# Multi-level attention with a feed-forward network: side products of TensorE in two parts

## The chip, the cores and the metric

One core of a Trainium2 chip runs the whole kernel. The time is that of one execution on the device in microseconds (us). Engines: TensorE (PE; its weight loads are PEld), VectorE (DVE), ScalarE (ACT), GpSimd (POOL), SyncE (SP, which starts most transfers).

## What is computed

The input is x of shape (8, 1024, 256) in float32. Cut to what matters:

```
for lvl in range(4):                       # strides 1, 2, 4, 8
    xs = x[:, ::2**lvl, :]                 # 1024, 512, 256, 128 tokens
    outs.append(mha(xs, in_proj_w[lvl], in_proj_b[lvl], out_w[lvl], out_b[lvl]))   # 16 heads of 16
current = outs[3]
for lvl in (2, 1, 0):
    current = upsample_linear(current, 2x) @ up_w[lvl].T + up_b[lvl] + outs[lvl]
x = layernorm(x + current)
h = silu(x @ w1 * s1) * (x @ w2 * s2)      # 256 -> 1024
h = gelu(h @ h1 * t1);  h = gelu(h @ h2 * t2)
x = layernorm(x + h @ w3 * s3)
```

## The kernel before

The program has two parts: attention for all eight batches (`attention`), and the feed-forward network (`ffn`). The change touches the first alone.

**Units and steps.** Attention of a batch is cut into 15 units, each of a level, four heads (more on the coarse levels, which have fewer tokens) and 512 queries. A unit runs over the key tiles of 128 tokens; one key tile is a step, and a batch has 85 steps (`STEPS`). A step has four maximum products ("max", L1313, 48 rows of the array each), two pairs of score products ("score", L1300, 50 rows each), and eight value products ("value", L1330). The maxima run 12 steps ahead of the scores (`LEAD`): VectorE reduces each of them out of PSUM (L1086), and the row maxima go into the scores as additional rows of the operands. ScalarE takes the exponentials of two score banks at a time (L982), and the value products of step s are issued two steps later.

**Rows of the array.** Heads lie in the upper or the lower 64 partitions (`rows_of`). Max 0 and max 2 of a fine step are in one half, max 1 and max 3 in the other (`maxima_of`), and each score pair has one product in either half.

**Side products.** Everything else that TensorE does in attention has a place at the end of a step (`SIDE = .85`): projections of q and k ("proj", 15 a batch), value projections ("v", 8), output products of the three coarse levels ("mid", 4), the up-projections ("lift", 2, and "row", 2), output products of the fine level ("out", 4), and transposes of the row maxima ("neg", 15). Apart from "neg" each is made of float32 operands cut into a high and a low part, three matmuls per product and 128 rows (`three`, L1190). Most have six matmuls of 512 columns or twelve of 256; the projections of level 3 are 24 of 128 columns.

**What sets the order.** `timeline` gives every task a time in steps, with the fraction as its place within the step. Each engine issues its tasks sorted by that time, with the engine's own additions in `LATER`. In a step TensorE thus has max 0 (.0), max 1 (.05), value (.1), max 2 (.3), score 0 (.4), max 3 (.6), score 1 (.7) and then the side product (.85). The order is unrolled for one batch, with a hardware loop over it, an opening ahead of it (the first batch's projections and maxima) and an end behind it.

**The ring.** Maxima and side products share three PSUM banks (`p_r`, `BANKS = 3`). `bank_plan` goes through them in order of time and gives each the bank that is promised free first; `HOLD` says for how long each kind keeps one (.45 of a step for a maximum, .7 to 1.1 for the others). Before TensorE writes into a bank it waits until the bank's last user was read: by VectorE for "max", "v", "row" and "out", by ScalarE for "proj", "neg", "mid" and "lift". The scores have four banks of their own and the value products one.

```
bank = min(range(BANKS), key=lambda bank: held[bank][0])
plan.bank[tuple(task)], plan.prev[tuple(task)] = bank, held[bank][1]
held = held[:bank] + [(at + HOLD[task[0]], [tuple(task)])] + held[bank + 1:]
```

Of the kernel before, what the change touches and what calls it, by code (L numbers as in the profile page):

```python
# [79 lines left out]
PROJ = [[Proj(2, t, m, 0) for t in range(2)] for m in range(2)]  # L80
# [3 lines left out]
PROJ_FIRST = {lvl: min(n for n, ps in enumerate(PROJ) if ps[0].lvl == lvl) for lvl in W_ORDER}  # L84
# [40 lines left out]
V_PAIRS = [[n for n, (l, kt) in enumerate(V_ORDER) if l == lvl][i:i + 2] for lvl in W_ORDER for i in range(0, tokens(lvl) // 128, 2)]  # L125
V_FIRST = {lvl: [ns[0] for ns in V_PAIRS].index(V_TILE[lvl]) for lvl in W_ORDER}
# [13 lines left out]
MID_FIRST, MID_DONE = {3: 0, 2: 1, 1: 2}, {3: 1, 2: 2, 1: 4}  # L140
# [92 lines left out]
def earlier(it):  # L233
# [30 lines left out]
def timeline(first):  # L264

    p = []
# [4 lines left out]
    side = places([(("neg", u), unit.end - LEAD) for u, unit in enumerate(UNITS)], taken)  # L271
# [9 lines left out]
    for lvl in W_ORDER:  # L281
# [5 lines left out]
        else:  # L287
# [17 lines left out]
    if first:  # L305
        at = [side[("proj", n)] for n in range(len(PROJ))]
# [86 lines left out]
def attention(nc, xt_in, xtok, wqkv_in, wo_in, cols, rows, ident_in, xt, wqkv, wo, scr, d75s, d25s, x1, wf, hi_scr, lo_scr, lo_max, f_hi, f_w3_lo):  # L393
# [31 lines left out]
    def bank_plan(p, held):  # L425

        plan = Plan({}, {})
        for at, *task in sorted(p, key=lambda task: (task[0], task[1:])):
            if task[0] in HOLD:
                bank = min(range(BANKS), key=lambda bank: held[bank][0])  # L430
                plan.bank[tuple(task)], plan.prev[tuple(task)] = bank, held[bank][1]
                held = held[:bank] + [(at + HOLD[task[0]], [tuple(task)])] + held[bank + 1:]
        return plan, held

    def one_batch_on(held):
# [12 lines left out]
    with ExitStack() as ctx:  # L448
# [153 lines left out]
        with nc.Block() as block:  # L602
# [573 lines left out]
            def _(pe):  # L1176
# [6 lines left out]
                lift_mm.open(pe)  # L1183
                row_mm.open(pe)

                def three(out, pairs):

                    terms = [t for (a_h, a_l), (b_h, b_l) in pairs for t in ((a_h, b_h), (a_l, b_h), (a_h, b_l))]
                    for n, (a, c) in enumerate(terms):
                        ins = pe.matmul(out, a, c, start=n == 0, stop=n == len(terms) - 1)  # L1190
                    return ins

                def both(hi, lo, *at):

                    return hi[at], lo[at]
# [1 line left out]
                every = slice(None)  # L1197

                def steps(tasks, iteration, plan):
                    for task in tasks:  # L1200
                        kind, k, n = task
                        it = iteration(k)
                        if kind in HOLD:
                            p_a = p_r[:, plan.bank[task], :]
                        for was, at, m in plan.prev.get(task, ()):

                            {"max": max_read, "proj": qk_read, "neg": neg_read, "v": v_done, "mid": mid_read, "lift": lift_read, "row": row_read, "span": span_read,
                             "out": out_read}[was].wait(pe, iteration(at), m + 1)
                        if kind == "proj":
                            lvl = PROJ[n][0].lvl  # L1210
                            size = min(W, tokens(lvl))
                            if n == 0:
                                x_lo_done.wait(pe, it, 1)
                            if n == PROJ_FIRST[0]:
                                x_lo_done.wait(pe, it, 2)
                            if n == PROJ_FIRST[lvl]:
                                w_lo_done.wait(pe, it, W_ORDER.index(lvl) + 1)
                            for i, (_, t, m, blk) in enumerate(PROJ[n]):
                                tok = slice(blk * W, blk * W + size)
                                ins = three(p_a[:, i * size:(i + 1) * size],  # L1220
                                            [(both(w_hi, w_lo, every, slice(at, at + 128)), both(x_hi, x_lo, every, c, tok))
                                             for c in range(2) for at in (c * 512 + t * 256 + m * 128,)])
                            ins.then_inc(qk_mm.sem, 1)
                        elif kind == "neg":
                            if n < FIRST_FINE:
                                max_read.wait(pe, it, MAX_AT[n + 1])
# [3 lines left out]
                                ins = pe.transpose(p_a[0:HG, q * 128:(q + 1) * 128], row_max[:, n % RING, q, :], ident[:, :])  # L1230
                            ins.then_inc(neg_mm.sem, 1)
                        elif kind == "v":
                            if n == V_FIRST[0]:
                                x_lo_done.wait(pe, it, 2)
                            for i, tile in enumerate(V_PAIRS[n]):
# [4 lines left out]
                            ins.then_inc(v_mm.sem, 1)  # L1240
                        elif kind == "mid":
                            lvl, ms = MIDS[n]
                            S, at = tokens(lvl), A_AT[lvl]
                            if n == MID_FIRST[lvl]:
                                a_lo_done.wait(pe, it, CUT_DONE[lvl])
                                o_lo_done.wait(pe, it, O_ORDER.index(lvl) + 1)
                            for i, m in enumerate(ms):
                                ins = three(p_a[:, i * S:(i + 1) * S], [(both(o_hi, o_lo, every, slice(c * E + m * 128, c * E + m * 128 + 128)),
                                                                         both(a_hi, a_lo, every, c, slice(at, at + S))) for c in range(2)])
                            ins.then_inc(mid_mm.sem, 1)  # L1250
                        elif kind == "lift":
                            lvl = O_ORDER[n]
                            S, at = tokens(lvl), A_AT[lvl]
                            c_lo_done.wait(pe, it, n + 1)
                            for m in range(2):
                                ins = three(p_a[:, m * S:(m + 1) * S], [(both(o_hi, o_lo, every, slice(WUP + c * E + m * 128, WUP + c * E + m * 128 + 128)),
                                                                         both(a_hi, a_lo, every, c, slice(at, at + S))) for c in range(2)])
                            ins.then_inc(lift_mm.sem, 1)
                        elif kind == "row":
                            if n == 0:  # L1260
# [5 lines left out]
                            ins.then_inc(row_mm.sem, 1)  # L1266
                        elif kind == "out":
                            if n % 2 == 0:
                                a_lo_done.wait(pe, it, len(CUTS) - 1 + n // 2)
                            if n == 0:  # L1270
                                o_lo_done.wait(pe, it, 4)
                            for q in range(2):
# [3 lines left out]
                            ins.then_inc(out_mm.sem, 1)  # L1276
# [533 lines left out]
```

## Time and profile before

| what | us |
| --- | --- |
| median of 3 runs | 4003.92 |
| lowest and highest | 3999.56, 4011.51 |
| profiled execution | 4005.5 |
| its span, first to last instruction | 4003.7 |
| TensorE busy in the span | 3642.2 (91%) |
| ScalarE busy | 2595.1 (65%) |
| VectorE busy | 2552.1 (64%) |

The page's slices cut the span into 40 equal parts of about 100 us; each digit is a busy share in tenths. The windows view gives, for one or more stretches of time, the busy time of each engine in it with the number of its instructions, the granted TensorE clock, and the DMA's share and rate; its last row sums over all stretches and divides by their number. Where a group below has a row that begins with "sum", the stretches were chosen by one rule, which the group's line names, over 300 to 2600 us, and what stands for one step is that sum divided by the number of stretches.

### The profile page before, as it was taken

The page shows a single profiled execution, that of the slowest core. Times are in us where ns is not written, and L with a number is a line of the kernel's source. Part 1 is how long each engine was busy: PE and PEld are TensorE (multiplying, and loading weights), DVE is VectorE, ACT ScalarE, POOL GpSimd, SP SyncE. Part 2 cuts the span into 40 slices and gives each one's busy share as a digit, 9 for nine tenths or more (in the row PEclk, how much of TensorE's full clock was granted, in tenths as well). Part 3 has the DMA queues.
Part 4 walks back from the last instruction along what each step waited for, and adds up shares of the span by engine and source line. Part 5 has one row for each costly group of instructions (what it writes and reads, how often), then busy time and mean ns, then how long its engine had stood idle before and what let it go on. Part 6 is the DMA issues. An engine that isn't in the chain of part 4 may idle for free. (4 is left out here: it accounts for less than half of the span.)

```text
span 4003.7 us, 70655 instructions
## 1 busy us (share of the span) xinstructions
PE 3642.2 (91%) x20993; PEld 1954.6 (49%) x20993; DVE 2552.1 (64%) x4806; ACT 2595.1 (65%) x3273; POOL 1051.4 (26%) x1024
## 2 busy tenths in 40 slices
PE   5899889989989989989988988869999999999998
PEld 3333333333333323333333332258878787887887
DVE  5778978878878887887897898523333333333333
ACT  2779778868868868877877978734444344443443
POOL 2233434434444343343443342210000000000000
PEclk6989989989989989998998999979999999999999
DMA  4423423422332332333332344210000000000000
GB/s 138 156 70 98 123 77 91 118 81 86 105 95 87 105 107 79 103 95 93 89 117 72 99 123 135 75 51 12 12 12 13 21 11 12 12 11 13 21 11 11
DMA packets 231920, 284.40 MB, mean 71 GB/s; under 512 B 53524, under 2 KB 189908, under 8 KB 230384
## 3 DMA queue, kind: packets, MB, share of 16 engines
q1 hardware_dynamic: 222272, 270.54, 22.5%
q10 hardware_dynamic: 9216, 8.39, 0.6%
q8 instruction: 236, 3.87, 0.4%
q14 instruction: 196, 1.61, 0.1%
HBM read 166.63 MB, written 108.00 MB: 69 GB/s over the span
## 5 line engine op out<-in xcount | busy, mean ns | idle before, releaser
L982 ACT ACTIVATE a_probs<-a_p_s,a_unit_now 128x1024 f32<-128x1024 f32 x1360 | 1448.7, 1111 | 351.9 <-PE a_p_s L1300 345.3
L1086 DVE TENSOR_REDUCE a_part_max<-a_p_r 128x1 f32<-128x512 f32 x2048 | 1301.6, 676 | 270.9 <-PE a_p_r L1313 266.4
L1313 PE MATMUL a_p_r<-a_k_st,a_q_st 48*128 48x512 f16 (+2 forms) x2944 | 921.0, 383 | 209.5 <-DVE a_part_max L1086 126.2
L1313 PEld LDWEIGHTS a_p_r<-a_k_st,a_q_st 48*128 48x128 f16 x2944 | 229.1, 94 | 1239.6 <-DVE a_part_max L1086 871.3
L1642 PE MATMUL p_h<-f_h_hi,f_w_hi 128*128 128x512 f32 x2048 | 807.3, 394 | 24.0 <-issue 24.0
L1642 PE MATMUL p_h<-f_h_lo,f_w_hi 128*128 128x512 f32 x2048 | 803.2, 392 | 0.0
L1330 PE MATMUL a_p_o<-a_probs,a_v_aug 128*17 128x512 f32 (+2 forms) x5888 | 747.5, 588 | 3.5 <-ACT a_raw L992 2.8
L1300 PE MATMUL a_p_s<-a_q_st,a_k_st 50*128 50x512 f16 (+2 forms) x2944 | 694.9, 376 | 25.9 <-ACT a_probs L982 24.0
L1613 DVE TENSOR_TENSOR f_h_lo<-f_h_f,f_h_hi 128x512 fp32r<-128x512 f32 x256 | 177.1, 692 | 697.2 <-ACT f_h_hi L1539 697.2
L1537 ACT ACTIVATE f_h_f<-p_h,f_sc 128x512 f32<-128x512 f32 x256 | 176.6, 690 | 556.7 <-PE p_h L1642 556.6
L1086 DVE TENSOR_REDUCE a_row_max<-a_p_r 128x1 f32<-128x512 f32 (+2 forms) x672 | 427.2, 676 | 98.2 <-PE a_p_r L1313 95.9
L1642 PEld LDWEIGHTS p_h<-f_h_hi,f_w_hi 128*128 128x128 f32 x2048 | 388.5, 190 | 107.9 <-issue 26.4
L1642 PEld LDWEIGHTS p_h<-f_h_lo,f_w_hi 128*128 128x128 f32 x2048 | 388.6, 190 | 80.1
L1483 POOL TENSOR_TENSOR f_rstd<-f_var_eps,f_minus_half 128x1 f32<-128x1 f32 x64 | 35.6, 556 | 1325.9 <-DVE f_var_eps L1604 1325.9
L837 POOL TENSOR_TENSOR a_qk_room<-a_qk_room 128x512 f16<-128x512 f32 x114 | 132.1, 1159 | 381.3 <-ACT a_qk_room L969 381.3
L859 POOL TENSOR_TENSOR a_neg_bf<-a_neg_f,a_neg_bf 4x512 f16<-4x512 f32 x120 | 138.3, 1153 | 308.8 <-ACT a_neg_bf L976 308.8
L1642 PE MATMUL p_h<-f_xt_hi,f_w_hi 128*128 128x512 f32 x512 | 200.3, 391 | 1.4 <-DVE f_xt_lo L1565 1.4
L1642 PE MATMUL p_h<-f_xt_lo,f_w_hi 128*128 128x512 f32 x512 | 200.1, 391 | 0.0
L1300 PEld LDWEIGHTS a_p_s<-a_q_st,a_k_st 50*128 50x128 f16 x2944 | 155.7, 95 | 90.1 <-ACT a_probs L982 59.7
L1581 DVE SCALAR_TENSOR_TENSOR f_h_f<-p_h,f_sc,f_gate 128x512 f32<-128x512 f32 x128 | 96.1, 751 | 158.6 <-PE p_h L1642 138.8
L1330 PEld LDWEIGHTS a_p_o<-a_probs,a_v_aug 128*17 128x17 f32 x5888 | 105.4, 96 | 175.0 <-issue 121.9
L863 POOL TENSOR_TENSOR a_attn<-a_raw,a_attn 128x512 f32<-128x512 f32 x120 | 152.9, 1274 | 126.5 <-DVE a_attn L1138 126.5
(131 smaller groups left out, 4533.6 us busy)
## 6 DMA issues: line engine op xcount, KB each, us to landing
qk_scratch<-a_qk_room SPq DMA_DIRECT2D x288, 128.0 KB
a_w_lo<-wqkv_inner SPq DMA_DIRECT2D x30, 768.0 KB, 4.3
a_q_st<-qk_scratch SPq DMA_DIRECT2D x64, 192.0 KB, 3.7
a_k_st<-qk_scratch SPq DMA_DIRECT2D x64, 192.0 KB, 4.8
a_a_lo<-a_attn SPq DMA_DIRECT2D x384, 32.0 KB, 2.0
a_o_lo<-wo_inner SPq DMA_DIRECT2D x24, 512.0 KB, 3.7
a_qk_room<-wf SPq DMA_DIRECT2D x22, 512.0 KB, 3.8
w_lo_scratch<-a_qk_room SPq DMA_DIRECT2D x22, 512.0 KB, 2.7
```

The costliest lines, as they stand in the source:

```text
L837: pool.tensor_tensor(out=pieces[:, 1, :], in0=qk[:, 0:size], in1=pieces[:, 0, :], op=ALU.subtract).then_inc(qk_lo.sem, 1)
L859: pool.tensor_tensor(out=neg_bf[:, n % 2, 1, :], in0=neg_f[:, :], in1=neg_bf[:, n % 2, 0, :], op=ALU.subtract).then_inc(neg_b.sem, 1)
L863: pool.tensor_tensor(out=attn[:, n % RING, :], in0=raw[:, n % 2, :], in1=attn[:, n % RING, :], op=ALU.mult)\
L982: act.activation(probs[:, s % 2, 2 * p:2 * p + 2, :], p_s[:, 2 * p:2 * p + 2, :], ACT.Exp, scale=unit_now[:, lvl:lvl + 1]).then_inc(exp_do ...
L1086: dve.reduce_max(out, src, AX.X).then_inc(max_read.sem, 1)
L1300: ins = pe.matmul(p_s[:, bank_of(j), i * size:(i + 1) * size], k_st[rows_of(j, ROWS + 2), key_at:key_at + 128], q_st[rows_of(j, ROWS + 2), ...
L1313: ins = pe.matmul(p_a[:, r * size:(r + 1) * size], q_st[rows_of(j, ROWS), query_at:query_at + 128], k_st[rows_of(j, ROWS), key_at:key_at + ...
L1330: ins = pe.matmul(p_o[32 * j:32 * j + HD + 1, at], v_aug[:, V_TILE[lvl] + kt, unit.head + j * parts + i, :], probs[:, n % 2, bank_of(j), a ...
L1537: act.activation(h_f[:, v % 2, :], p_h[:, v % 4, :], ACT.Gelu, scale=sc[:, 8 + v:9 + v]).then_inc(deep_read.sem, 1)
L1581: dve.scalar_tensor_tensor(out=h_f[:, v % 2, :], in0=p_h[:, (2 * v + 1) % 4, :], scalar=sc[:, 8 + v:9 + v], in1=gate[:, v % 2, :], op0=ALU ...
L1613: dve.tensor_tensor(out=h_lo[:, (half + v // 8) % 2, v % 8, :], in0=h_f[:, v % 2, :], in1=h_hi[:, (half + v // 8) % 2, v % 8, :], op=ALU.s ...
L1642: ins = pe.matmul(out, a, c, start=first and n == 0, stop=last and n == len(terms) - 1)
```

## The change

The six kinds of side products in `PARTED` (all but "neg") are issued in two parts. The first part has its place half a step ahead of the second (`FIRST_PART = -.5`), at .35 of the step, between max 2 and score 0. A product that covers two or more tiles of its bank is cut by tiles; one that fills its bank with a single tile (512 columns) is cut by the two halves of its contraction, so that it accumulates in the same bank over both parts. All waits for inputs and for the bank are made by the first part, and the semaphore is counted by the second. The planner books the bank from the first part's time to the end it had before. The value projection of level 3 has one tile; its first part is empty.

```diff
+PARTED = ("proj", "v", "mid", "lift", "row", "out")
+FIRST_PART = -.5
...
     p += [(at, kind, n) for (kind, n), at in side.items()]
+    p += [(at + FIRST_PART, "first_" + kind, n) for (kind, n), at in side.items() if kind in PARTED]
...
+    if kind == "first_out":
+        return LAST_OUT[n] + FIRST_PART
...
-        for at, *task in sorted(p, key=lambda task: (task[0], task[1:])):
-            if task[0] in HOLD:
+        for at, kind, k, n in sorted(p, key=lambda task: (task[0], task[1:])):
+            task = (kind.removeprefix("first_"), k, n)
+            if task[0] in HOLD and task not in plan.bank:
+                until = at + HOLD[task[0]] - (FIRST_PART if task[0] in PARTED else 0)
...
-                def three(out, pairs):
+                def three(out, pairs, first=True, last=True):
...
-                        ins = pe.matmul(out, a, c, start=n == 0, stop=n == len(terms) - 1)
+                        ins = pe.matmul(out, a, c, start=first and n == 0, stop=last and n == len(terms) - 1)
...
+                def half_of(things, second):
+
+                    middle = len(things) // 2
+                    return things[middle:] if second else things[:middle]
...
-                        for was, at, m in plan.prev.get(task, ()):
+                        for was, at, m in () if second and kind in PARTED else plan.prev.get(task, ()):
...
-                            for i, (_, t, m, blk) in enumerate(PROJ[n]):
+                            whole = len(PROJ[n]) > 1
+                            for i, (_, t, m, blk) in half_of(list(enumerate(PROJ[n])), second) if whole else enumerate(PROJ[n]):
...
-                                             for c in range(2) for at in (c * 512 + t * 256 + m * 128,)])
-                            ins.then_inc(qk_mm.sem, 1)
+                                             for c in (range(2) if whole else (int(second),)) for at in (c * 512 + t * 256 + m * 128,)],
+                                            whole or not second, whole or second)
+                            if second:
+                                ins.then_inc(qk_mm.sem, 1)
...
-                            for q in range(2):
+                            for q in (int(second),):
```

The other kinds are changed in the same way, each by its tiles or by its contraction.

## Rows read from the trace of the kernel before

**Rows 1.** The page: busy time of the engines, and its slices of TensorE.
```profile
PE 3642.2 (91%) x20993; PEld 1954.6 (49%) x20993; DVE 2552.1 (64%) x4806; ACT 2595.1 (65%) x3273; POOL 1051.4 (26%) x1024
...
PE   5899889989989989989988988869999999999998
```

**Rows 2.** Windows by stage: start:end length, busy us (instructions) per engine, clock, DMA.
```profile
120.00:1300.00 1180.00, 1067.67 (x7007) 394.83 (x7007) 957.53 (x1814) 937.48 (x1116) 467.33 (x436) 0.95 0.33 97
1300.00:2600.00 1300.00, 1172.32 (x7746) 420.48 (x7743) 1052.14 (x1999) 1042.04 (x1231) 503.43 (x469) 0.95 0.33 99
```

**Rows 3.** Waits of 300 to 2600 us: who waited for whom, us, times, longest.
```profile
ACT a_probs L982 <- PE a_p_s L1300: 314.2, 303, 4.4
...
DVE a_part_max L1086 <- PE a_p_r L1313: 242.1, 279, 3.6
...
PE a_p_r L1313 <- DVE a_part_max L1086: 116.4, 178, 8.0
```

**Rows 4.** Windows over 190 steps without side products, value to value.
```profile
sum 618.82, PE 505.19 PEld 126.48 DVE 539.00 ACT 465.14 POOL 278.85; mean PE 2.66 PEld 0.67 DVE 2.84 ACT 2.45 POOL 1.47
```

**Rows 5.** Windows of 97 products of six 512s: whole steps; leads; blocks.
```profile
sum 388.93, PE 381.31 PEld 154.60 DVE 287.73 ACT 351.35 POOL 108.34; mean PE 3.93 PEld 1.59 DVE 2.97 ACT 3.62 POOL 1.12
...
sum 100.99, PE 96.20 PEld 29.24 DVE 97.13 ACT 78.48 POOL 21.97; mean PE 0.99 PEld 0.30 DVE 1.00 ACT 0.81 POOL 0.23
...
sum 153.93, PE 153.93 PEld 101.66 DVE 87.92 ACT 153.93 POOL 55.73; mean PE 1.59 PEld 1.05 DVE 0.91 ACT 1.59 POOL 0.57
```

**Rows 6.** Windows of 117 products of twelve 256s: whole steps; first lead, leads; blocks.
```profile
sum 508.64, PE 490.73 PEld 252.52 DVE 392.35 ACT 389.25 POOL 189.21; mean PE 4.19 PEld 2.16 DVE 3.35 ACT 3.33 POOL 1.62
...
353.36:354.12 0.76, 0.76 (x10) 0.22 (x7) 0.34 (x1) 0.73 (x2) 0.76 (x1) 1.00 0.20 43
...
sum 144.34, PE 128.92 PEld 36.15 DVE 122.73 ACT 88.73 POOL 64.53; mean PE 1.10 PEld 0.31 DVE 1.05 ACT 0.76 POOL 0.55
...
sum 199.83, PE 199.83 PEld 183.95 DVE 145.22 ACT 186.28 POOL 80.19; mean PE 1.71 PEld 1.57 DVE 1.24 ACT 1.59 POOL 0.69
```

**Rows 7.** Timeline of one lead, from max 2 on: start, us, engine, line, xcount.
```profile
1303.02 0.39 PE L1313 MATMUL a_p_r<-a_k_st,a_q_st 48*128 48x512 f16 x1
...
1303.02 0.60 PE L1300 MATMUL a_p_s<-a_q_st,a_k_st 50*128 50x512 f16 x2
...
1303.25 0.38 PE L1313 MATMUL a_p_r<-a_k_st,a_q_st 48*128 48x512 f16 x1
1303.44 1.29 DVE L1086 TENSOR_REDUCE a_part_max<-a_p_r 128x1 f32<-128x512 f32 x2 [0.59 <-PE a_p_r L1313]
1303.46 0.38 PE L1300 MATMUL a_p_s<-a_q_st,a_k_st 50*128 50x512 f16 x2
...
1303.78 0.39 PE L1190 MATMUL a_p_r<-a_o_hi,a_a_hi 128*128 128x256 f32 x1
```

**Rows 8.** Timeline of a projection's block: its first two matmuls, its last, next maximum.
```profile
1318.27 0.50 PE L1190 MATMUL a_p_r<-a_x_hi,a_w_hi 128*128 128x512 f32 x1
1318.61 0.40 PE L1190 MATMUL a_p_r<-a_x_hi,a_w_lo 128*128 128x512 f32 x1
...
1319.53 0.40 PE L1190 MATMUL a_p_r<-a_x_lo,a_w_hi 128*128 128x512 f32 x1
...
1319.86 0.39 PE L1313 MATMUL a_p_r<-a_k_st,a_q_st 48*128 48x512 f16 x1
```

**Rows 9.** Windows: 7 blocks of six 256s; 7 leads ahead of 24 matmuls.
```profile
sum 6.34, PE 6.34 PEld 5.39 DVE 4.99 ACT 6.34 POOL 6.34; mean PE 0.91 PEld 0.77 DVE 0.71 ACT 0.91 POOL 0.91
...
sum 5.32, PE 5.32 PEld 1.52 DVE 2.35 ACT 4.79 POOL 0.00; mean PE 0.76 PEld 0.22 DVE 0.34 ACT 0.68 POOL 0.00
```

**Rows 10.** Timeline: split weights of a level, and its first projection.
```profile
1271.09 3.44 POOL L826 TENSOR_TENSOR a_w_lo<-a_w_lo,a_w_hi 128x1536 fp32r<-128x1536 f32 x1
...
1275.60 0.33 PE L1190 MATMUL a_p_r<-a_x_hi,a_w_hi 128*128 128x128 f32 x1
```

More of the change, by code:

```diff
@@ L427, in bank_plan @@
         plan = Plan({}, {})
[L428 to L429 removed]
+        for at, kind, k, n in sorted(p, key=lambda task: (task[0], task[1:])):
+            task = (kind.removeprefix("first_"), k, n)
+            if task[0] in HOLD and task not in plan.bank:
+                until = at + HOLD[task[0]] - (FIRST_PART if task[0] in PARTED else 0)
                 bank = min(range(BANKS), key=lambda bank: held[bank][0])
[L431 to L432 removed]
+                plan.bank[task], plan.prev[task] = bank, held[bank][1]
+                held = held[:bank] + [(until, [task])] + held[bank + 1:]
         return plan, held
@@ L1199, in steps @@
                 def steps(tasks, iteration, plan):
-                    for task in tasks:
-                        kind, k, n = task
+                    for kind, k, n in tasks:
                         it = iteration(k)
+                        second = not kind.startswith("first_")
+                        kind = kind.removeprefix("first_")
+                        task = (kind, k, n)
                         if kind in HOLD:
                             p_a = p_r[:, plan.bank[task], :]
-                        for was, at, m in plan.prev.get(task, ()):
+                        for was, at, m in () if second and kind in PARTED else plan.prev.get(task, ()):
                             {"max": max_read, "proj": qk_read, "neg": neg_read, "v": v_done, "mid": mid_read, "lift": lift_read, "row": row_read, "span": span_read,
@@ L1211, in steps @@
                             size = min(W, tokens(lvl))
-                            if n == 0:
+                            if n == 0 and not second:
                                 x_lo_done.wait(pe, it, 1)
-                            if n == PROJ_FIRST[0]:
+                            if n == PROJ_FIRST[0] and not second:
                                 x_lo_done.wait(pe, it, 2)
-                            if n == PROJ_FIRST[lvl]:
+                            if n == PROJ_FIRST[lvl] and not second:
                                 w_lo_done.wait(pe, it, W_ORDER.index(lvl) + 1)
-                            for i, (_, t, m, blk) in enumerate(PROJ[n]):
+                            whole = len(PROJ[n]) > 1
+                            for i, (_, t, m, blk) in half_of(list(enumerate(PROJ[n])), second) if whole else enumerate(PROJ[n]):
                                 tok = slice(blk * W, blk * W + size)
@@ L1232, in steps @@
                         elif kind == "v":
-                            if n == V_FIRST[0]:
+                            if n == V_FIRST[0] and not second:
                                 x_lo_done.wait(pe, it, 2)
-                            for i, tile in enumerate(V_PAIRS[n]):
+                            for i, tile in half_of(list(enumerate(V_PAIRS[n])), second):
                                 kt = V_ORDER[tile][1]
@@ L1239, in steps @@
                                                                         for c in range(2)])
-                            ins.then_inc(v_mm.sem, 1)
+                            if second:
+                                ins.then_inc(v_mm.sem, 1)
                         elif kind == "mid":
@@ L1243, in steps @@
                             S, at = tokens(lvl), A_AT[lvl]
-                            if n == MID_FIRST[lvl]:
+                            if n == MID_FIRST[lvl] and not second:
                                 a_lo_done.wait(pe, it, CUT_DONE[lvl])
                                 o_lo_done.wait(pe, it, O_ORDER.index(lvl) + 1)
-                            for i, m in enumerate(ms):
+                            whole = len(ms) > 1
+                            for i, m in half_of(list(enumerate(ms)), second) if whole else enumerate(ms):
                                 ins = three(p_a[:, i * S:(i + 1) * S], [(both(o_hi, o_lo, every, slice(c * E + m * 128, c * E + m * 128 + 128)),
-                                                                         both(a_hi, a_lo, every, c, slice(at, at + S))) for c in range(2)])
-                            ins.then_inc(mid_mm.sem, 1)
+                                                                         both(a_hi, a_lo, every, c, slice(at, at + S))) for c in (range(2) if whole else (int(second),))],
+                                            whole or not second, whole or second)
+                            if second:
+                                ins.then_inc(mid_mm.sem, 1)
                         elif kind == "lift":
@@ L1253, in steps @@
                             S, at = tokens(lvl), A_AT[lvl]
-                            c_lo_done.wait(pe, it, n + 1)
-                            for m in range(2):
+                            if not second:
+                                c_lo_done.wait(pe, it, n + 1)
+                            for m in (int(second),):
                                 ins = three(p_a[:, m * S:(m + 1) * S], [(both(o_hi, o_lo, every, slice(WUP + c * E + m * 128, WUP + c * E + m * 128 + 128)),
                                                                          both(a_hi, a_lo, every, c, slice(at, at + S))) for c in range(2)])
-                            ins.then_inc(lift_mm.sem, 1)
+                            if second:
+                                ins.then_inc(lift_mm.sem, 1)
                         elif kind == "row":
-                            if n == 0:
+                            if n == 0 and not second:
                                 c_lo_done.wait(pe, it, 3)
-                            for q in range(2):
+                            for q in (int(second),):
                                 at = A_AT[1] + (2 * n + q) * 128
@@ L1265, in steps @@
                                                                          both(o_hi, o_lo, every, slice(WUP + c * E, WUP + c * E + E))) for c in range(2)])
-                            ins.then_inc(row_mm.sem, 1)
+                            if second:
+                                ins.then_inc(row_mm.sem, 1)
                         elif kind == "out":
-                            if n % 2 == 0:
+                            if n % 2 == 0 and not second:
                                 a_lo_done.wait(pe, it, len(CUTS) - 1 + n // 2)
-                            if n == 0:
+                            if n == 0 and not second:
                                 o_lo_done.wait(pe, it, 4)
-                            for q in range(2):
+                            for q in (int(second),):
                                 tok = slice((2 * n + q) * 128, (2 * n + q + 1) * 128)
@@ L1275, in steps @@
                                                                         for c in range(2)])
-                            ins.then_inc(out_mm.sem, 1)
+                            if second:
+                                ins.then_inc(out_mm.sem, 1)
                         elif kind == "span":
```

## The prediction

> **What bounds the kernel now.** I read the page's slices first, then windows by stage, then the waits of the attention part, then windows over single steps, and last the timeline of one step.
>
> The slices show two parts [rows 1]: attention up to about 2640 us, and the feed-forward network behind it, which the change does not touch. In attention TensorE is busy 1067.67 of 1180 us and 1172.32 of 1300 us, VectorE 957.53 and 1052.14, ScalarE 937.48 and 1042.04 [rows 2]. No engine is full, so the time is made of stretches with different limits. The waits of 300 to 2600 us tell which two engines trade places: VectorE waits 242.1 us for maximum products of TensorE, and TensorE waits 116.4 us for VectorE's reductions [rows 3].
>
> Windows that each hold one step (from the first value product to the next step's) show the two kinds. A step without any side product takes 618.82 / 190 = 3.26 us with TensorE busy 2.66 and VectorE 2.84 [rows 4]: VectorE is the nearer limit and TensorE has room. A step with a side product of six 512-column matmuls takes 388.93 / 97 = 4.01 us with TensorE busy 3.93 [rows 5], one of twelve 256-column matmuls 508.64 / 117 = 4.35 us with TensorE 4.19 [rows 6]. There TensorE is the limit, and VectorE is idle for about 1.0 us (4.01 - 2.97, 4.35 - 3.35). So time that the change adds to TensorE in a side step counts in full, unless a wait goes in return.
>
> **Inside a side step.** From max 2 of the step to the side product (the lead) TensorE issues max 2, two scores, max 3, two scores. These use 48 or 50 rows each, in the lower or the upper half of the array, and pairs in different halves run at once: a maximum and a score start together at 1303.02, and six products take three slots of about 0.22 us [rows 7]. An unhindered lead takes 0.76 us (first row of the lead's windows [rows 6]). On average it takes 100.99 / 97 = 1.04 us and 144.34 / 117 = 1.23 us [rows 5, 6]. The difference, 0.28 and 0.47 us, is waiting, and VectorE is busy through nearly the whole lead (97.13 of 100.99 us [rows 5]): TensorE waits for a bank of the three-bank ring to be read. The block itself, up to the next maximum, takes 153.93 / 97 = 1.59 us and 199.83 / 117 = 1.71 us.
>
> **The change, part by part.** Nothing is computed more or less. Every product of the six kinds is cut in two. The second part stays behind score 1. The first part goes to the place between max 2 and the first score pair of the same step.
>
> (a) Switches. A side product uses all 128 rows. Around a block the rows show a transition three times: 0.32 us from the start of the last score to the first side matmul, where a slot is 0.22 [rows 7]; 0.34 us from first to second side matmul, where the next ones follow every (1319.53 - 1318.61) / 4 = 0.23 us; and 0.33 us from the last to the next maximum, where 0.23 would do [rows 8]. That is 0.10 + 0.11 + 0.10 = 0.31 us per block, and a cut product has two blocks. Half of six 512s is then 0.34 + 0.23 + 0.33 = 0.90 us, and half of twelve 256s is what the undivided product of six 256s takes, 6.34 / 7 = 0.91 us [rows 9].
>
> (b) Lost pairing. With the first part between them, max 2 no longer shares a slot with a score. The remaining five (score, score, max 3, score, score) still need three slots, since one half has three of them. So one slot of 0.22 us is added.
>
> (c) The new order, with no wait at all, is: max 2 to first part 0.32, first part 0.90, five half-row products and switch 0.76, second part 0.90: 2.88 us for the 512s, 2.90 for the 256s. Before, unhindered: 0.76 + 1.59 = 2.35. So the bare price is 2.88 - 2.35 = 0.53 us per cut product.
>
> (d) Waits that go. By the planner's rule (the bank that is promised free first) the order of banks in a lone side step stays: max 3 took max 0's bank and the side product max 1's; now the first part takes max 0's and max 3 takes max 1's. VectorE reads two maxima back to back in 1.29 us [rows 7], 0.65 us each, so max 0's bank is free about 0.65 us before max 1's. If the side product now starts on average 1.04 us after max 2, the first part can start at about 1.04 - 0.65 = 0.39, against 0.32 unhindered; and max 3, behind the first part, finds its bank read long ago. So the waits of the lead shrink from 0.28 us to 0.07. The bank is held half a step longer, but its promised end is the same as before, so the maxima of the next step keep their banks; I cost that at nothing. If that is wrong, one maximum per product waits for one more reduction, 0.65 us, and this is inside the upper end.
>
> Against the measured lead plus block: 512s: 2.88 + 0.07 - (1.04 + 1.59) = +0.32 us; 256s: 2.90 + 0.07 + 0.10 (the block's average above its unhindered 1.60 stays) - (1.23 + 1.71) = +0.13 us. The level-3 projection (24 small matmuls) has a lead without any wait, 5.32 / 7 = 0.76 us [rows 9], so it pays the full 0.5. The 128-column products of twelve are few (16) and the single value tile isn't cut: nothing.
>
> (e) Counts from the code: per batch 14 of the 512s (12 of them projections), 17 of the 256s (9 of them projections and values), one of 24. The first batch's projections and values run in the opening, where no scores run and TensorE is half idle (slices 5 and 8 [rows 1]): nothing. So 12 x 7 + 2 x 8 = 100, 9 x 7 + 8 x 8 = 127, and 7. Sum: 100 x 0.32 + 127 x 0.13 + 7 x 0.5 = 32 + 16.5 + 3.5 = 52 us.
>
> (f) Waits that move. Each wait for inputs goes with the first part, some 0.7 us earlier, and behind it on TensorE now stand the step's scores, for which ScalarE waits. The tightest that I found is a level's first projection: the split weights are ready at 1271.09 + 3.44 = 1274.53, the product starts at 1275.60 [rows 10]: 1.07 us of room, still enough. Consumers wait for the second part, which moves only by the added time. ScalarE gets the step's first score pair a whole first part later (about 1.0 us) and then the second pair at once; value products use exponentials of the step before last, so I cost it at nothing. Without that cover it would be up to 1.0 us in the steps of six, ScalarE being busy 3.62 of 4.01 us there [rows 5].
>
> (g) VectorE. Max 2 and max 3 used to come together; now a first part lies between, so it idles between them too, and again before the next step's maxima. It leaves a side step with nothing queued before and after. So the steps without a side product (PE idle 0.60 us each [rows 4]) do not get shorter.
>
> The profiled execution took 4005.5 us for a span of 4003.7; its time is 1.6 above the median of 4003.92. 4005.5 + 52 = 4057.5, less 1.6: 4056 us.
>
> **A rule weighed.** The rows show about 0.31 us of transition per block in (a). The Trainium skill, TensorE: Matmul & The Clock Gate (section Part 2: What happens when you issue a matmul), says that one matmul's drain is covered by the next one's fill, so that matmuls behind each other cost their columns alone; its page TensorEngine Tiling (Array Packing), section Key Properties, says that a change of tiling mode drains the array, which speaks against this change. The trace agrees with the second. By the first alone an extra block would be free: a rival below.
>
> **The rivals.**
> - Full price (chance 0.17): the waits of the lead come back elsewhere, before max 3 or in the next maxima, because VectorE has the same four reductions and a bank is tied up longer. Then 234 x 0.53 = 124 us: 4126 us. For: VectorE is busy 90% of the leads ((97.13 + 122.73) of (100.99 + 144.34) us). Against: the whole step gets longer, so it has more time per reduction.
> - Faster (0.20): VectorE is fed more evenly, since the longest run of TensorE without a maximum halves, and what it no longer idles shortens the steps without side products. For: 242.1 us of VectorE waiting for maxima [rows 3], about 1.0 us per side step. It decides once it brings more than 52 / 234 = 0.22 us per cut product. If half of TensorE's visible waits for reductions go, 116.4 / 2 x 2620 / 2300 = 66 us, the sum is -14: 3990 us; if all of them, 3923. Against: (g); the two gaps together are as long as the one.
> - No net change (0.13): the added time gives VectorE and ScalarE room for what they owe, and the following steps return about all of it: 4004 us.
> - Transitions free (0.05): the first rule above as a mechanism here; the second block costs no transition, so 234 x 0.31 = 73 us less than the forecast: 3983 us.
> - Forecast (0.45).
>
> **How the numbers follow.** A measurement of this kernel tells about 0.3% (12 us) from no change. Slower: forecast 0.45, full price 0.17, a part of "no net change" 0.03, together 0.65. Within 0.3%: 0.10 from "no net change" and the edges. Faster: 0.20 + 0.05, together 0.25. The forecast's own range is 4030 to 4085. The 8-in-10 range leaves out the far half of the full price and of the faster rival: 3980 to 4125.
>
> **What would show it.** Right: windows from max 2 to the next step's maximum of about 2.95 us for the 512s (2.63 before) and 3.05 for the 256s (2.94); steps without side products still 3.26 us; two VectorE gaps in a side step; VectorE's total wait for maxima above 242 us. (a) and (b) are wrong if those windows fall to 2.6; (d) is wrong if the part from the first part's end to the second's start is well over 0.76 us; (g) is wrong, and the faster rival right, if the steps without side products fall below 3.1 us. Wait rows of a score for ScalarE would show that (f) was costed too low.

## The result

The changed kernel takes 4126.46 us (median of 4 runs, 4123.45 to 4129.45) against 4007.7 us before (4 runs): a ratio of 1.03, interval 1.0287 to 1.0313. It is slower by 3%. The sign was forecast, the size was not: 52 us were forecast and 119 measured, which is the time worked out for the "full price" rival. All times here are of fast runs; one of the tenth run's four, 4529.39 us at a granted clock of 0.732, was slow and is left out.

The profiled execution took 4125.4 us (span 4123.6), 119.9 more than before. Nearly all of it lies in attention: from the first step's value products to the last step's it takes 2603.2 us (113.2 to 2716.4) and took 2486.8 (110.1 to 2596.9). The work is the same, 20993 matmuls. From the page after (busy time, then idle before the exponentials and before the reductions, with what ended it):

```profile
PE 3738.8 (91%) x20993; PEld 1964.3 (48%) x20993; DVE 2571.6 (62%) x4806; ACT 2592.8 (63%) x3273; POOL 1049.5 (25%) x1024
...
L989 ACT ACTIVATE a_probs<-a_p_s,a_unit_now 128x1024 f32<-128x1024 f32 x1360 | 1448.2, 1111 | 510.9 <-PE a_p_s L1325 507.2
L1093 DVE TENSOR_REDUCE a_part_max<-a_p_r 128x1 f32<-128x512 f32 x2048 | 1319.2, 678 | 348.1 <-PE a_p_r L1338 342.6
```

TensorE's busy time rose by 96.6 us with the same matmuls [rows 1]: products that used to run in pairs now run alone, and a matmul at a border takes longer. VectorE and ScalarE run the same number of instructions (busy 19.5 us more and 2.3 less) and wait longer for TensorE. TensorE, in turn, waits as long as before for reductions, here over 300 to 2700 us (116.4 us before [rows 3], over 2300 us):

```profile
ACT a_probs L989 <- PE a_p_s L1325: 465.0, 366, 5.7
...
DVE a_part_max L1093 <- PE a_p_r L1338: 315.7, 448, 3.5
...
PE a_p_r L1338 <- DVE a_part_max L1093: 112.8, 179, 8.9
```

Now the windows, of the changed kernel from 300 to 2700 us, which answer to [rows 4 to 6]. First the steps without a side product (190), then the 97 products of six 512s: whole steps; from max 2 to the first part; from the first part's end to the second part.

```profile
sum 621.38, PE 506.26 PEld 127.24 DVE 542.79 ACT 502.31 POOL 279.36; mean PE 2.66 PEld 0.67 DVE 2.86 ACT 2.64 POOL 1.47
...
sum 425.58, PE 411.86 PEld 149.04 DVE 294.18 ACT 321.22 POOL 125.86; mean PE 4.25 PEld 1.54 DVE 3.03 ACT 3.31 POOL 1.30
...
sum 43.01, PE 34.99 PEld 9.22 DVE 40.40 ACT 32.06 POOL 9.23; mean PE 0.36 PEld 0.10 DVE 0.42 ACT 0.33 POOL 0.10
...
sum 73.33, PE 73.33 PEld 21.99 DVE 17.59 ACT 31.34 POOL 37.66; mean PE 0.76 PEld 0.23 DVE 0.18 ACT 0.32 POOL 0.39
```

A step without a side product takes 621.38 / 190 = 3.27 us (3.26 before). A step of six 512s takes 425.58 / 97 = 4.39 us (4.01), so 0.38 more. Its first part starts 0.44 us after max 2, and the half-row products between the parts take 0.76 us with no wait at all.

The 117 products of twelve 256s (whole steps, max 2 to first part), the 7 of twenty-four, and the 7 of the single value tile:

```profile
sum 548.77, PE 531.29 PEld 262.07 DVE 403.58 ACT 355.28 POOL 179.08; mean PE 4.54 PEld 2.24 DVE 3.45 ACT 3.04 POOL 1.53
...
sum 63.34, PE 46.91 PEld 12.01 DVE 52.16 ACT 33.50 POOL 15.83; mean PE 0.40 PEld 0.10 DVE 0.45 ACT 0.29 POOL 0.14
...
sum 37.50, PE 37.50 PEld 23.53 DVE 15.44 ACT 25.83 POOL 12.79; mean PE 5.36 PEld 3.36 DVE 2.21 ACT 3.69 POOL 1.83
...
sum 27.41, PE 24.65 PEld 9.58 DVE 18.71 ACT 25.44 POOL 17.54; mean PE 3.52 PEld 1.37 DVE 2.67 ACT 3.63 POOL 2.51
```

They take 4.69 us, 5.36 us and 3.92 us. Before, the last two were 4.89 and 3.21 us:

```profile
sum 34.25, PE 34.25 PEld 22.42 DVE 14.76 ACT 27.25 POOL 12.85; mean PE 4.89 PEld 3.20 DVE 2.11 ACT 3.89 POOL 1.84
...
sum 22.45, PE 22.45 PEld 9.01 DVE 18.02 ACT 17.38 POOL 17.57; mean PE 3.21 PEld 1.29 DVE 2.57 ACT 2.48 POOL 2.51
```

For the 256s the average before, 4.35 us [rows 6], can't be set against 4.69 as it stands: its 117 windows hold the very end of attention, which in the changed kernel falls behind 2700 us. There TensorE stands idle for 6.74 us ahead of the last output product. Below are one of six steps that also hold a small "span" product, their sum, and this last window, all of the kernel before:

```profile
548.41:555.80 7.40, 7.32 (x37) 3.55 (x37) 4.08 (x11) 2.14 (x3) 2.36 (x8) 0.54 0.06 13
...
sum 45.78, PE 45.34 PEld 21.44 DVE 24.40 ACT 13.11 POOL 14.18; mean PE 7.56 PEld 3.57 DVE 4.07 ACT 2.19 POOL 2.36
...
2585.29:2596.93 11.65, 4.59 (x26) 2.96 (x25) 0.00 (x0) 4.28 (x5) 3.79 (x3) 0.69 0.49 140
```

Without the last window a step of twelve 256s took (508.64 - 11.65) / 116 = 4.28 us, so it grew by 0.41 us. The six steps with a "span" product run at a granted clock of 0.50 to 0.54 in both kernels and grew from 7.63 to 8.61 us, by 0.98; the other 110 took 4.10 us, and such steps now take 4.48, 0.38 more, as much as the 512s.

Summed over the counts of (e): 100 x 0.38 + 127 x 0.41 + 7 x 0.47 + 7 x 0.71 = 38 + 52 + 3 + 5 = 98 us. The 128-column products of twelve add about 9 x 0.64 = 6, the steps with a transpose alone (405.69 / 109 against 395.69 / 108 = 0.06 us) 7, the others 4, the opening 3. That places 118 of 120 us.

One side step in the timeline of the changed kernel shows the layout, TensorE only:

```profile
1342.78 0.39 PE L1338 MATMUL a_p_r<-a_k_st,a_q_st 48*128 48x512 f16 x1
1343.24 0.50 PE L1197 MATMUL a_p_r<-a_a_hi,a_o_hi 128*128 128x512 f32 x1
...
1344.14 0.60 PE L1325 MATMUL a_p_s<-a_q_st,a_k_st 50*128 50x512 f16 x3
1344.37 0.38 PE L1338 MATMUL a_p_r<-a_k_st,a_q_st 48*128 48x512 f16 x1
1344.59 0.38 PE L1325 MATMUL a_p_s<-a_q_st,a_k_st 50*128 50x512 f16 x1
1344.90 0.51 PE L1197 MATMUL a_p_r<-a_a_hi,a_o_hi 128*128 128x512 f32 x1
```

Max 2 stands alone at 1342.78. The first part starts 0.46 us later, not 0.32: it waits for the bank. Then five half-row products take three slots, at 1344.14, 1344.37 and 1344.59.

### The profile page after: what moved, and what is told of

It reads as the page before. It is cut to its first block and busy times, and to the rows that moved or that the text cites. A ratio compares the mean times of both kernels' runs of the same rounds, so it can differ in the third digit from the quotient of the medians.

```text
span 4123.6 us, 70663 instructions
## 1 busy us (share of the span) xinstructions
PE 3738.8 (91%) x20993; PEld 1964.3 (48%) x20993; DVE 2571.6 (62%) x4806; ACT 2592.8 (63%) x3273; POOL 1049.5 (25%) x1024
## 5 line engine op out<-in xcount | busy, mean ns | idle before, releaser
L989 ACT ACTIVATE a_probs<-a_p_s,a_unit_now 128x1024 f32<-128x1024 f32 x1360 | 1448.2, 1111 | 510.9 <-PE a_p_s L1325 507.2
L1093 DVE TENSOR_REDUCE a_part_max<-a_p_r 128x1 f32<-128x512 f32 x2048 | 1319.2, 678 | 348.1 <-PE a_p_r L1338 342.6
L1325 PE MATMUL a_p_s<-a_q_st,a_k_st 50*128 50x512 f16 (+2 forms) x2944 | 654.6, 378 | 24.8 <-ACT a_probs L989 21.6
```

Source lines behind the costliest of these rows:

```text
L989: act.activation(probs[:, s % 2, 2 * p:2 * p + 2, :], p_s[:, 2 * p:2 * p + 2, :], ACT.Exp, scale=unit_now[:, lvl:lvl + 1]).then_inc(exp_do ...
L1093: dve.reduce_max(out, src, AX.X).then_inc(max_read.sem, 1)
L1325: ins = pe.matmul(p_s[:, bank_of(j), i * size:(i + 1) * size], k_st[rows_of(j, ROWS + 2), key_at:key_at + 128], q_st[rows_of(j, ROWS + 2), ...
```

## The experiments

Each ratio is to the kernel before, timed beside the run. A word for reading them: the 7 steps of twenty-four small matmuls never waited in the lead before, so they show the bare price of an order (not in runs 7 and 8, where they wait behind the product: 5.84 and 5.90 us against 4.89), and the steps of six 512s show price and waits together. A border is what the prediction calls a switch: the transition between products of 48 to 50 rows and products of 128.

**1. The two parts next to each other.**

```diff
-FIRST_PART = -.5
+FIRST_PART = -.01
```

> The first part stands directly ahead of the second (-.01 of a step instead of -.5), so nothing runs between them. Theory A (a second block pays about 0.31 us of switches, and max 2 loses the slot it shared with a score, 0.22 us, and only about half of that comes back as waits that go): neither price is paid, 4008 us within 12. Rival B (it is the cutting itself, the second task and its bookkeeping): stays near 4126 us.

4010.19 us, ratio 1.0006 (0.9996 to 1.0016). Cutting alone costs nothing, so B falls. All that follows is a matter of place.

**2 to 4. The first part at three other places in the step.**

```diff
-FIRST_PART = -.5
+FIRST_PART = -.2     # second run: behind max 3
+FIRST_PART = -.35    # third run: between score pair 0 and max 3
+FIRST_PART = -.65    # fourth run: between the value products and max 2
```

> The first part stands between max 3 and the second score pair (-.2). Max 2 and a score share a slot again, max 3 and a score too, and the second score pair the third: the lost slot is back, the second block stays. Theory A: about 250 x 0.22 = 55 us less than the changed kernel, about 4070 us. Rival C (what costs is that VectorE gets max 3 a whole part later and starves twice): max 3 comes at its old time, nearly all comes back, 4010 to 4030 us.

> The first part stands between the first score pair and max 3 (-.35). Max 2 shares a slot with a score, but max 3 and the second pair need two slots, and the second score of the first pair's half one of its own: four slots in all, as in the changed kernel. Theory A: 4126 us within 15. Rival D (the late first score pair starves ScalarE, and that sets the loss): ScalarE has its pair at the old time, 4060 to 4090 us.

> The first part stands between the value products and max 2 (-.65). All six half-row products are together again in three slots, and one border of half-row products and full-row matmuls is gone, since the value products before it use all rows: Theory A: 4040 to 4070 us. Rival C (VectorE's supply): max 2 and max 3 both reach VectorE a whole part late, so the loss is as in the changed kernel or larger, 4126 us or more.

Measured: 4108.2 us (ratio 1.0243, 1.0226 to 1.026), 4082.81 us (1.0186, 1.0169 to 1.0203) and 4126.09 us (1.0307, 1.0282 to 1.0331). Theory A, which I held, missed in all three, and not on one side. C's number was missed by the second run and met by the fourth (4126 us or more); D's range holds the third. The second run's windows (steps of twenty-four, steps of six 512s, lead of these):

```profile
sum 35.99, PE 35.99 PEld 22.89 DVE 14.78 ACT 28.00 POOL 12.82; mean PE 5.14 PEld 3.27 DVE 2.11 ACT 4.00 POOL 1.83
...
sum 425.24, PE 407.96 PEld 146.79 DVE 286.70 ACT 352.77 POOL 104.83; mean PE 4.21 PEld 1.51 DVE 2.96 ACT 3.64 POOL 1.08
...
sum 91.08, PE 73.86 PEld 20.29 DVE 87.98 ACT 68.10 POOL 18.15; mean PE 0.76 PEld 0.21 DVE 0.91 ACT 0.70 POOL 0.19
```

The lost slot is real: the steps of twenty-four go from 5.36 to 35.99 / 7 = 5.14 us, 0.22 less. But the 512s stay at 425.24 / 97 = 4.38, since their lead up to the first part is 0.94 us where the steps of twenty-four need 0.54: behind max 3, TensorE has to wait for two banks before the first part, as it did before the change. The third run's windows (steps and lead of the 512s):

```profile
sum 408.35, PE 407.86 PEld 141.53 DVE 294.79 ACT 349.06 POOL 108.66; mean PE 4.20 PEld 1.46 DVE 3.04 ACT 3.60 POOL 1.12
...
sum 53.46, PE 52.97 PEld 12.27 DVE 48.40 ACT 36.85 POOL 10.51; mean PE 0.55 PEld 0.13 DVE 0.50 ACT 0.38 POOL 0.11
```

Its price is that of the changed kernel (5.35 us in the steps of twenty-four), but the 512s take 4.21 us: their lead is 0.55 us against 0.53 unhindered, so the waits of the lead are gone. Collected, in us:

| first part | steps of twenty-four | steps of six 512s | median |
| --- | --- | --- | --- |
| none (before) | 4.89 | 4.01 | 4008 |
| before max 2 (-.65) | 5.04 | 4.33 | 4126 |
| before score pair 0 (-.5, the change) | 5.36 | 4.39 | 4126 |
| before max 3 (-.35) | 5.35 | 4.21 | 4083 |
| behind max 3 (-.2) | 5.14 | 4.38 | 4108 |

The second column orders the places otherwise than the third. So price alone (A) does not order the times. It takes both: a fixed price in slots and borders, and the waits that the new place takes away, leaves or adds. In the fourth run waits were added. First its TensorE waiting for reductions over 300 to 2600 us, 110.2 us in the changed kernel; then VectorE waiting for maxima over the same stretch, in the changed kernel and in the eleventh run:

```profile
PE a_p_r L1338 <- DVE a_part_max L1093: 169.1, 259, 8.3
...
DVE a_part_max L1093 <- PE a_p_r L1338: 306.9, 435, 3.5
...
DVE a_part_max L1094 <- PE a_p_r L1339: 262.7, 294, 3.8
```

VectorE's supply alone (C) does not order them either: VectorE waits 314.5 us in the second run, which is 18 us faster than the changed kernel with its 306.9, and only 262.7 in the eleventh, which is 28 us slower. D isn't shown: in the third run ScalarE has its first pair early, but the windows give the 512s' whole gain to the bank wait, and TensorE's waits of scores for ScalarE hardly move (9.5 us, 11.0 in the changed kernel).

**5 and 6. Both kernels with lighter reductions.**

```diff
+                            if parts == 1:
+                                src = p_a[:, 0:W // 2]
                             dve.reduce_max(out, src, AX.X).then_inc(max_read.sem, 1)
...
-                            act.activation(unit_now[:, lvls], unit_next[:, lvls], ACT.Copy, scale=HD ** -0.5 / 4)
+                            act.activation(unit_now[:, lvls], unit_next[:, lvls], ACT.Copy, scale=HD ** -0.5 / 64)
```

> The kernel before, with the maxima of levels 0 and 1 reduced over 256 of their 512 columns, and a smaller scale of the exponentials so that they stay finite: the values are not the reference's. VectorE is no limit any more, so the 0.28 to 0.34 us of waiting in the lead of a side step and most of the 0.6 us of idle TensorE in the other steps go. All theories: well below the kernel before, 3700 to 3850 us; its run is the base for the next one.

> The changed kernel with the same lighter reductions (values not the reference's). Theory A (fixed price of 0.52 us of TensorE per cut product, of which waits gave a part back): with no waits left to go the price is paid in full, about 234 x 0.52 = 122 us or a little more above the light kernel before. Rival C (VectorE starves in the changed order): with VectorE no limit the difference falls to less than half, under 60 us.

Both reduce the maxima of levels 0 and 1 over half of their columns, so their values are not the reference's. 3903.33 us (ratio 0.9746) and 3999.05 us (0.9976), a difference of 95.7 us where the real pair has 119. C falls (it asked for under 60). My number (122 or more) was too high, for a reason the windows give; steps and leads of six 512s, of the light kernel before:

```profile
sum 385.40, PE 369.67 PEld 150.19 DVE 195.44 ACT 356.49 POOL 129.68; mean PE 3.85 PEld 1.56 DVE 2.04 ACT 3.71 POOL 1.35
...
sum 100.15, PE 86.58 PEld 26.05 DVE 65.09 ACT 82.42 POOL 27.55; mean PE 0.90 PEld 0.27 DVE 0.68 ACT 0.86 POOL 0.29
```

The lead is still 100.15 / 96 = 1.04 us though VectorE does a third less: another wait took its place, a score's for ScalarE (93.9 us in this run, 16.2 before, over 300 to 2600 us). In the light changed kernel the lead is 0.32 us and the step 409.15 / 96 = 4.26, so 0.25 more than 4.01: the price of 0.53 less the whole 0.28 of waiting. So for the 512s the account of price and waits holds whichever engine is waited for. The light kernels also show that VectorE's load is worth only 104 us to the kernel before.

**7 and 8. The undivided product at another place.**

```diff
-    p += [(at, kind, n) for (kind, n), at in side.items()]
+    p += [(at + (MOVE if kind in MOVED else 0), kind, n) for (kind, n), at in side.items()]
+MOVED = ("proj", "v", "mid", "lift", "row", "out")
+MOVE = -.3     # seventh run: between score pair 0 and max 3
+MOVE = -.65    # eighth run: between the value products and max 2
```

> The kernel before with the undivided side product moved from behind score pair 1 to between score pair 0 and max 3 (.55 instead of .85 of a step). One block only, so no added switches; the half-row products on the two sides need two slots each, four in all, 0.21 us more. Theory A with the waits as the part cut there before max 3 showed them (0.02 us left of 0.28 to 0.34): 0.07 to 0.13 us less per product than before, 15 to 30 us faster than the kernel before, 3980 to 3995 us. Rival E (the waits only move behind the product): the slot is lost for nothing, 4008 + 225 x 0.21 = 4055 us.

> The kernel before with the undivided side product moved to between the value products and max 2 (.2 of the next place). One block, three slots, and one border less (the value products use all rows too, and that border cost nothing where the first part stood there): 0.1 to 0.2 us less of TensorE. Against it the waits, 0.27 us in the lead and about 0.13 ahead of the product when only its first part stood there. Theory A: 3990 to 4020 us. Rival C (VectorE gets max 2 and max 3 a whole product of 1.6 us late): 4060 us or more.

4170.04 us (ratio 1.0416, 1.0398 to 1.0433) and 4230.11 us (1.0557, 1.054 to 1.0575): the largest misses, and the most telling. The eighth run meets C's number (4060 us or more) and was not taken apart. In the seventh the waits of the lead did go (51.48 / 96 = 0.54 us), but the step of six 512s takes 448.85 / 96 = 4.68 us. The timeline of the seventh run, behind a product:

```profile
1353.28 0.39 PE L1315 MATMUL a_p_r<-a_k_st,a_q_st 48*128 48x512 f16 x1
1353.28 0.60 PE L1302 MATMUL a_p_s<-a_q_st,a_k_st 50*128 50x512 f16 x2
1353.51 0.38 PE L1315 MATMUL a_p_r<-a_k_st,a_q_st 48*128 48x512 f16 x1
1353.70 1.89 DVE L1088 TENSOR_REDUCE a_part_max<-a_p_r 128x1 f32<-128x512 f32 x3 [2.67 <-PE a_p_r L1315]
...
1354.45 0.39 PE L1315 MATMUL a_p_r<-a_k_st,a_q_st 48*128 48x512 f16 x1 [0.56 <-DVE a_part_max L1088]
```

Max 3 (1353.28) and the next max 0 (1353.51) go out at once; the next max 1 (1354.45) must have max 3's bank and waits 0.56 us for its reduction. The bank comes back 1.17 us after its maximum was issued. In the kernel before the product stands exactly in that gap: 1.59 us of TensorE's work between max 3 and the next maxima cover the reductions of max 2 and max 3. Moved ahead of max 3, it no longer covers that reduction.

**9. Only the projections cut.**

```diff
-FIRST_PART = -.5
+FIRST_PART = {"proj": -.5, "v": -.01, "mid": -.01, "lift": -.01, "row": -.01, "out": -.01}
```

> Only the projections have their first part half a step ahead; the other five kinds are undivided as before. Theory A adds up by product: 84 of six 512s at 0.38 us, 14 of twelve 256s at 0.31, 7 of 24 at 0.47: 32 + 4 + 3 = 39 us more than the kernel before, 4045 to 4052 us. Rival G (the loss comes where side products follow each other step by step, as the value and output products do, or out of the wait of the empty first part): under 20 us more, below 4028 us.

4061.66 us, ratio 1.0139 (1.0121 to 1.0156): 54 us of the 119, with 105 of the 234 products that (e) counts. The loss is spread over the kinds, so G falls. It is 15 us above my sum of 39: seven of the fourteen 256s are steps with a "span" product, which pay 0.98 us instead of 0.31 (5 us), and about 7 us lie in the steps with a transpose alone, as in the changed kernel.

**10 and 11. The second part moved back instead of the first forward.**

```diff
-FIRST_PART = -.5
+FIRST_PART = -.001
+SECOND_LATER = .22    # tenth run, behind the next max 1; eleventh: .35, behind the value products
-                iterations(pe, steps)
+                iterations(pe, steps, {kind: SECOND_LATER for kind in PARTED})
```

> Cut in two, but the first part stays behind score pair 1 and the second goes behind the next step's max 0 and max 1, ahead of its value products (only on TensorE; the consumers keep their order). No slot is lost, the borders keep their number (maxima to value products before, maxima to second part now), a block more costs 2 x 0.90 - 1.59 = 0.21 us. VectorE gets max 0 and max 1 0.9 us earlier. Theory A with the waits of the lead (0.28 to 0.34 us) as what can go: 0.07 to 0.13 us per product less than before, 3980 to 3995 us. Rival H (max 1 waits for the reduction of max 3, 1.1 us, which only the whole block covered): 4030 to 4060 us.

> As the run before, with the second part behind the next step's value products and ahead of max 2. Theory A: a block more (0.21 us) and 0.1 us of border, waits of the lead gone: 3995 to 4015 us. Rival C (max 2 reaches VectorE 0.9 us late in every side step): 4040 us or more.

4078.8 us (ratio 1.0174, 1.0154 to 1.0195) and 4154.09 us (1.0361, 1.0343 to 1.0378). The eleventh meets C's number (4040 us or more), though VectorE's waits there speak against C. In the tenth run the price is small (35.27 / 7 = 5.04 us in the steps of twenty-four, 0.15 more than before), but the 512s take 418.20 / 96 = 4.36 us. The windows from max 2 to the first part and over the next two maxima:

```profile
sum 92.02, PE 85.07 PEld 25.70 DVE 72.78 ACT 70.12 POOL 15.47; mean PE 0.89 PEld 0.27 DVE 0.76 ACT 0.73 POOL 0.16
...
sum 56.89, PE 45.31 PEld 14.28 DVE 32.24 ACT 56.89 POOL 14.96; mean PE 0.47 PEld 0.15 DVE 0.34 ACT 0.59 POOL 0.16
```

The lead still waits 0.96 - 0.76 = 0.20 us, and the two maxima, sent half a product earlier, now take 0.59 us where 0.32 suffices: they meet banks that are not read yet. The direction of H is right, its number was too low. No order that I ran beats the kernel before.

## Why the prediction was right or wrong

- **Which engine limits which step: right.** The steps without side products stayed at 3.27 us, so (g) held. The faster rival had nothing to stand on, and nor had "no net change": nothing came back in the steps behind.
- **(a) to (c), the price: right.** The steps of twenty-four, which never waited, show it bare: two blocks instead of one, 2 x 1.49 - 2.83 = 0.15 us; lead and middle 0.32 + 0.76 - 0.76 = 0.32 us. Together 0.47 (forecast 0.5). For the 512s the parts are 0.90 and 0.90 us and the middle 0.76, as forecast.
- **(d), the waits that go: the step that failed.** It let the leads shrink to 0.39 us for both kinds and took the whole difference as won. For the 512s it was nearly right: the first part starts at 0.44 us, and the step grew by 0.38 us, not 0.32. The 256s were forecast at 0.13 us and grew by 0.41: 36 of the 67 us that were missing.

  Half of that is the average that I took, 1.23 us of lead over 117 windows, as if all of its 0.47 us of waiting were waits for banks. Seven windows are odd. In the last one of attention the lead is 7.84 us, no wait that a cut could win back. In the six with a "span" product leads average 2.51 us and blocks 2.82, at half the clock, and these lost 0.98 us each. The other 110 average 1.10 and 1.64; with these the same sum gives 2.90 + 0.07 + 0.04 - (1.10 + 1.64) = 0.27 us. Most of the other half is the start of the first part, 0.49 us in the plain steps and not 0.39: that makes 0.37 us, against 0.38 measured. The sign that I named for (d), the part between the two halves, looked at the wrong place: it stayed at 0.76 us.
- **Products left out of the sum.** I let the 128-column products pay nothing because their waits were long; they grew by 0.64 us each. The single value tile "isn't cut", but its empty first part still makes TensorE wait for the bank ahead of the scores: 3.92 us against 3.21. Where the first part stands behind max 3 (run 2) the same step takes 3.22 us. Both together are 11 us.
- **(f), moved waits: right.** The waits of the scores for ScalarE did not grow (21.6 us in the whole run, 24.0 before), although ScalarE waits 507.2 us for scores instead of 345.3. It had the room.
- **The rivals.** "Full price" gave the right total for the wrong reason: it said that the waits come back behind the first part. They did not come back there (0.76 us, no wait), nor in the rest of the step (4.39 - 0.44 - 0.90 - 0.76 - 0.90 = 1.39 us, against 4.01 - 1.04 - 1.59 = 1.38 before). Nearly half of them stayed ahead of it, and some 25 us came from products and steps that no rival priced. That the total met 4126 us is luck. "Transitions free", as a mechanism for free blocks, is refuted: two blocks of 0.90 us stand against one of 1.59.

A last point on the borders. Between half-row and full-row products the rows show 0.10 us each way. The Trainium skill, TensorEngine Tiling (Array Packing), section Key Properties, says that changing the tiling mode drains the array. The trace agrees there, but not everywhere: in the fourth run the first part stands behind the value products (128 rows, 17 columns), and the steps of twenty-four pay 5.04 - 4.89 = 0.15 us, which is the second block alone. That border cost nothing that can be seen in the step.

What stays open: about 11 of the 120 us are placed but not explained, 0.06 us in each step with a transpose alone and less in the others. They may come from ring positions that the new booking shifts; no run shows it. Nor does a run show why the first part still waits 0.12 to 0.17 us for its bank instead of 0.07.

## What to carry to other kernels

A long product at the end of a step is not only a cost on TensorE: it is the time in which another engine empties the banks that the next products need, so before cutting or moving it, look at what was issued just ahead of it and when that bank is wanted again. Cutting costs a fixed amount per piece (a block's start, its borders, any pairing of half-array products that it breaks), and only the wait directly ahead of it can be won back. When such waits are averaged over many windows, look at the spread first, and leave out what has no counterpart: seven odd windows of 117 made half of the gap between 0.13 and 0.41 us, and one of them, kept in the comparison afterwards, would have hidden 9 us of the loss.

## What the runs showed of the hardware

- Two half-row products of 512 columns in different halves of the array share a slot of 0.22 us; a full-row product between them breaks the pair, 0.22 us (steps of twenty-four, 5.36 against 5.14 us).
- A block of 512-column matmuls on full rows costs 2 x 0.90 - 1.59 = 0.21 us more when it is cut in two, and a block of 128-column ones 0.15.
- From the start of a 512-column maximum to the start of the next product in its bank 1.17 us passed where VectorE was free (seventh run: 0.42 until its reduction starts; a reduction takes 0.68 on average).
- In the steps with a "span" product TensorE's granted clock was 0.50 to 0.54, the lower level of 1.2 GHz, and cutting the 256s there cost 0.98 us instead of 0.38.
